# First layers and query/key projections in two halves of 256 columns in place of one matmul of 512

## Chip, cores and metric

One core of a Trainium2 chip runs the whole kernel. The metric is the device time of one execution in microseconds (us), lower is better; the number for the kernel before is the median of three runs. The profile is one further execution of the same program.

## What is computed

The input has 16 rows of 512 tokens with 256 features, float32. For each row:

```python
x = x + attn_block(layernorm(x))      # pre-norm attention, 16 heads of 16, window of 15 tokens, then a 256-1024-256 GELU layer
x = x + ffn_block(layernorm(x))       # main 256-1024-256 GELU layer, plus 2 of 8 experts (256-1024-256), chosen per row
# attn_block: qkv = h @ qkv_w + qkv_b ; windowed softmax(q k / 4) v ; @ proj_w
# ffn_block : a * main + (1 - a) * sum_k gate_k * (gelu(x @ W1e[k] + b1e[k]) @ W2e[k] + b2e[k])
```

So each row passes four two-layer networks of hidden width 1024: one in the attention block (kind "m" below) and three in the second block (kind "f": main and the two chosen experts).

## The kernel before

The program is written by hand, engine by engine, with semaphores. TensorE (PE) multiplies, ScalarE (ACT) applies GELU and rounds, VectorE (DVE) makes the low parts and does softmax and norms, GpSimd (POOL) splits the expert weights, SyncE (SP) issues the DMAs.

Precision: every float32 operand of a large product is kept as a pair, a rounded part `hi` and a rest `lo`, and each product is the sum of three matmuls, hi·hi, hi·lo and lo·hi (function `three`, L258 to L262; all large matmuls carry the line L261). Each matmul loads its stationary operand of 128 columns (LDWEIGHTS, rows "PEld") and streams its moving operand past it. In the trace a name such as `psB<-z_hi,wx_hi` gives the result, the moving and the stationary operand; for the second layers (`psB<-wx_hi,hr_hi`) the weights move and the hidden values are stationary.

The hidden width is cut into 32 chunks of 128 a row: 24 of kind "f" and 8 of kind "m". A written-out order (`ORDER`) runs, for slot q of a row, `chunk_up` of chunk q (first layer: 2 parts of the contraction x 3 products = 6 matmuls of 512 token columns into one PSUM bank) and then `chunk_down` of chunk q-2 (second layer: 4 groups of 128 tokens x 3 products = 12 matmuls with 256 weight columns moving). Between the two lie GELU (L984), rounding (L988) and the low part `hr_lo` (L632). The operands of the first layers are `zT` (kind "m") and `z3` (kind "f"); their weights are `wf1`, `wm1` and, for experts, a ring `wx` of four that POOL fills (L522, L524) from `raw`.

Between the chunks the order puts the attention of the row: `project_qk` (queries and keys, 4 per row, each 6 matmuls of 512 columns), `values` (12 matmuls of 256 columns in a half, `wv` moving), `scores` (L1272), transposes (L1161, L1289), `attend` (L1311) and `project` (24 matmuls of 256 columns, `wproj` moving). Three unused tensors (`shift_values`, `shift_z`, `shift_hr`, of 128, 64 and 224 bytes) move the addresses of what is allocated after them.

The change's and the prediction's steps touch `three`, `chunk_up`, `project_qk`, and, as neighbours on PE, `chunk_down`, `values` and `project`.

Of the kernel before, what the change touches and what calls it, by code (L numbers as in the profile page):

```python
# [5 lines left out]
P = 128  # L6
# [16 lines left out]
def build(nc, x, qkv_w, qkv_b, proj_w, proj_b, g1, b1, g2, b2, fc1_w, fc1_b, fc2_w, fc2_b,  # L23
# [4 lines left out]
    ROWS, T, D = x.shape  # L28
    HID = fc1_w.shape[1]
    E = w_gate.shape[1]  # L30
    KD, KH, NT = D // P, HID // P, T // P
# [32 lines left out]
    with ExitStack() as ctx:  # L64
# [3 lines left out]
        def pair(name, shape):  # L68
            return [sb(f"{name}_hi", shape, f32r), sb(f"{name}_lo", shape, f32r)]

        def signal(name, per=1, unit=1):
            return Signal(ctx.enter_context(nc.semaphore(f"s_{name}")), per, unit)
# [4 lines left out]
        wqk = pair("wqk", [P, KD, 2 * D])  # L77
# [19 lines left out]
        zT = pair("zT", [P, KD, T])  # L97
        z3 = pair("z3", [P, KD, T])
# [53 lines left out]
        psB = ctx.enter_context(nc.psum_tensor("psB", [P, 4, 512], f32))  # L152
        psA = ctx.enter_context(nc.psum_tensor("psA", [P, 4, 512], f32))
# [98 lines left out]

        router, lg_s, m8_s, idx_s, tw_s, tanh_s = (signal(n) for n in ("router", "lg", "m8", "idx", "tw", "tanh"))
        gate_s, b1x_in, b2x_in, b2_s = signal("gate", 2), signal("b1x_in", 2, 16), signal("b2x_in", 2, 16), signal("b2", 2)

        def split_value(n):
            return n + 1

        def three(eng, dst, a, b, start, stop):
            for n, (u, v) in enumerate(((0, 0), (0, 1), (1, 0))):  # L260
                last = eng.matmul(dst, a[u], b[v], start=start and n == 0, stop=stop and n == 2)  # L261
            return last  # L262

        def chunk_weights(m):
            if m < KH:
                return ([[w[:, k, m * P:(m + 1) * P] for w in wm1] for k in range(KD)], [w[:, m, :] for w in wm2])
            s = (m - KH) % RING
            return ([[w[:, s, k * P:(k + 1) * P] for w in wx] for k in range(KD)], [w[:, s, KD * P:] for w in wx])
# [42 lines left out]
        def fc(t, m):  # L311
            return CHUNK["f", t - 1, m]

        def mc(t, m):
            return CHUNK["m", t, m]
# [842 lines left out]
        def _(pe):  # L1158
# [4 lines left out]

            def chunk_up(t, kind, m):
                if kind == "m":
                    ps, z, off = psA, zT, 0
                    w1 = [[w[:, k, m * P:(m + 1) * P] for w in wf1] for k in range(KD)]
                    if m >= 2:
                        pe.wait_ge(gelu.sem, mc(t, m - 2) + 1)
                else:  # L1170
                    ps, z, off = psB, z3, 0
                    w1, _ = chunk_weights(m)
                    if m == 0:
                        pe.wait_ge(z3_lo.sem, z3_lo.all(t - 1))
                    if m >= KH:
                        pe.wait_ge(w_lo.sem, w_lo.at(t - 1, m - KH))
                    if m >= 2:
                        pe.wait_ge(gelu.sem, fc(t, m - 2) + 1)
                    elif t > 1:
                        pe.wait_ge(gelu.sem, fc(t - 1, NCH - 2 + m) + 1)  # L1180
                    elif m == 1:
                        pe.wait_ge(vs_s.sem, vs_s.all(1))
                for k in range(KD):
                    if kind == "m" and m == 0:
                        pe.wait_ge(t2_lo.sem, t2_lo.at(t, k))
                    last = three(pe, ps[:, m % 2, :], w1[k], [a[:, k, off:off + T] for a in z], k == 0, k == KD - 1)
                last.then_inc(up.sem, 1)

            def chunk_down(t, kind, m):
# [32 lines left out]
            def project_qk(t, c, which, bank):  # L1222
                col = which * D + c * P
                for k in range(KD):
                    if c == 0:
                        pe.wait_ge(t1_lo.sem, t1_lo.at(t, k))
                    last = three(pe, psA[:, bank, :], [w[:, k, col:col + P] for w in wqk], [z[:, k, :] for z in zT], k == 0, k == KD - 1)
                last.then_inc(qk.sem, 1)

            def values(t, n, parts=range(2)):  # L1230
# [123 lines left out]
            for h in range(2):  # L1354
                pe.wait_ge(z1_s.sem, z1_s.at(0, 2 * h + 1))
                for c in range(KD):
                    for i in HALVES[h]:
                        last = pe.transpose(psA[:, c, i * P:(i + 1) * P], tn[:, i, c * P:(c + 1) * P], ident[:, :])
# [10 lines left out]
            pe.wait_ge(p_lo.sem, split_value(2))  # L1369
            pe.wait_ge(small_t.sem, 1)  # L1370
            project_qk(0, 0, 0, 3)
            pe.wait_ge(p_lo.sem, split_value(3))
            project_qk(0, 0, 1, 2)
            values(0, 0)

            for t in range(ROWS + 1):
                f = t - 1
                for q in range(NQ + 2):
                    if q < NQ and there(ORDER[q][0], t):
                        chunk_up(t, *ORDER[q])  # L1380
# [14 lines left out]
                    elif q == 2:  # L1395
                        if t:
                            pe.wait_ge(vs_s.sem, vs_s.all(t))
                        else:
                            pe.wait_ge(kT_s.sem, kT_s.at(0, 0))
                        project_qk(t, 1, 1, 2)  # L1400
                    elif q == 3:
                        if t:
# [104 lines left out]
```

## Time and profile before

| | |
|---|---|
| median of 3 runs | 1864.18 us (1863.76 to 1865.44) |
| the profiled execution's own time | 1867.85 us |
| its span, first to last instruction | 1865.8 us |
| PE busy | 1851.9 us, 99% of the span |
| DVE, ACT, POOL busy | 1366.5, 1169.1, 870.2 us (73, 63, 47%) |
| PE matmuls, weight loads | 19591, 19591 |
| granted TensorE clock, mean | 0.998 of full speed |

Matmuls are pipelined: the duration of one in the profile (0.39 us for 512 columns, 0.28 us for 256) overlaps the next. What a matmul costs in a stream is the distance from its start to the next start, and that is read from the timeline.

### The profile page before, as it was taken

The page shows a single profiled execution, that of the slowest core. Times are in us where ns is not written, and L with a number is a line of the kernel's source. Part 1 is how long each engine was busy: PE and PEld are TensorE (multiplying, and loading weights), DVE is VectorE, ACT ScalarE, POOL GpSimd, SP SyncE. Part 2 cuts the span into 40 slices and gives each one's busy share as a digit, 9 for nine tenths or more (in the row PEclk, how much of TensorE's full clock was granted, in tenths as well). Part 3 has the DMA queues.
Part 4 walks back from the last instruction along what each step waited for, and adds up shares of the span by engine and source line. Part 5 has one row for each costly group of instructions (what it writes and reads, how often), then busy time and mean ns, then how long its engine had stood idle before and what let it go on. Part 6 is the DMA issues. An engine that isn't in the chain of part 4 may idle for free.

```text
span 1865.8 us, 49302 instructions
## 1 busy us (share of the span) xinstructions
PE 1851.9 (99%) x19591; PEld 1672.5 (90%) x19591; DVE 1366.5 (73%) x2226; ACT 1169.1 (63%) x1832; POOL 870.2 (47%) x788
## 2 busy tenths in 40 slices
PE   8999999999999999999999999999999999999999
PEld 7899898998989989899898998989999898999998
DVE  7677877778777686776867767687777877778644
ACT  6675665757557575665756657566575655657554
POOL 6545362552715437164362634636255371552725
PEclk9999999999999999999999999999999999999999
DMA  4231311303122032220313103131131311203121
GB/s 135 60 91 40 97 58 38 88 29 97 58 57 75 24 97 58 74 64 27 96 49 87 57 28 99 41 97 47 38 95 35 97 58 47 80 29 97 46 63 57
DMA packets 147437, 121.88 MB, mean 65 GB/s; under 512 B 17964, under 2 KB 139784, under 8 KB 147208
## 3 DMA queue, kind: packets, MB, share of 16 engines
q1 hardware_dynamic: 146512, 117.90, 22.1%
q8 instruction: 155, 2.54, 0.6%
q10 hardware_dynamic: 696, 0.83, 0.1%
q14 instruction: 74, 0.61, 0.1%
HBM read 85.52 MB, written 8.39 MB: 50 GB/s over the span
## 4 chain that ended last, share of the span: by engine, by line
PE 98%; DVE 1%; issue 0%; POOL 0%; DMA 0%; ACT 0%; SPq 0%; DVEq 0%; POOLq 0%; ACTq 0%
PE psB L261 58%; PE psA L261 28%; PE psA L1272 4%; PE psA L1289 3%; PE psA L1161 2%; PE psA L1311 2%; PE psB L1346 0%; PE psA L1327 0%; DMA xin<-in_L_attn_x 0%; POOL wf_lo L513 0%; DVE smax L745 0%; PE psB L1272 0%; PE psB L1289 0%; DVE smax L732 0%; DVE pr L749 0%
## 5 line engine op out<-in xcount | busy, mean ns | idle before, releaser
L632 DVE TENSOR_TENSOR hr_lo<-hf,hr_hi 128x512 fp32r<-128x512 f32 x512 | 504.6, 986 | 413.4 <-ACT hr_hi L988 413.1
L522 POOL TENSOR_SCALAR wx_hi<-raw 128x512 fp32r<-128x512 f32 x256 | 200.2, 782 | 650.8 <-DMA raw<-in_L_ffn_W2e 389.0
L988 ACT ACTIVATE hr_hi<-hf 128x512 fp32r<-128x512 f32 x512 | 323.4, 632 | 263.1 <-PE psB L261 179.9
L524 POOL TENSOR_TENSOR wx_lo<-raw,wx_hi 128x512 fp32r<-128x512 f32 x256 | 406.5, 1588 | 21.4
L984 ACT ACTIVATE hf<-psB,b1x 128x512 f32<-128x512 f32 x256 | 175.5, 686 | 178.1 <-PE psB L261 176.2
L261 PE MATMUL psB<-wx_hi,hr_hi 128*128 128x256 f32 x1016 | 283.8, 279 | 0.3
L261 PE MATMUL psB<-wx_hi,hr_lo 128*128 128x256 f32 x1016 | 281.5, 277 | 0.0
L261 PE MATMUL psB<-wx_lo,hr_hi 128*128 128x256 f32 x1016 | 281.5, 277 | 0.0
L261 PE MATMUL psB<-z_hi,wx_hi 128*128 128x512 f32 x512 | 212.1, 414 | 0.0
L261 PE MATMUL psB<-z_lo,wx_hi 128*128 128x512 f32 x512 | 201.7, 394 | 0.0
L261 PE MATMUL psB<-z_hi,wx_lo 128*128 128x512 f32 x512 | 201.5, 394 | 0.0
L261 PEld LDWEIGHTS psB<-wx_hi,hr_hi 128*128 128x128 f32 x1016 | 190.8, 188 | 11.6 <-DVE hr_lo L632 0.9
L261 PEld LDWEIGHTS psB<-wx_lo,hr_hi 128*128 128x128 f32 x1016 | 191.0, 188 | 8.8
L261 PEld LDWEIGHTS psB<-wx_hi,hr_lo 128*128 128x128 f32 x1016 | 190.7, 188 | 0.0
L984 ACT ACTIVATE hf<-psB,smallT 128x512 f32<-128x512 f32 x128 | 88.4, 690 | 120.3 <-PE psB L261 118.3
L461 POOL TENSOR_SCALAR ve<-mv 128x2 f32<-128x2 f32 (+1 forms) x94 | 25.2, 268 | 279.7 <-DVE mv L627 278.2
L261 PE MATMUL psA<-wf_hi,hr_hi 128*128 128x256 f32 x512 | 142.3, 278 | 0.0
L261 PE MATMUL psB<-wm_hi,hr_hi 128*128 128x256 f32 x512 | 142.2, 278 | 0.0
L261 PE MATMUL psA<-wf_lo,hr_hi 128*128 128x256 f32 x512 | 141.7, 277 | 0.0
L261 PE MATMUL psB<-wm_hi,hr_lo 128*128 128x256 f32 x512 | 141.7, 277 | 0.0
L261 PE MATMUL psA<-wf_hi,hr_lo 128*128 128x256 f32 x512 | 141.7, 277 | 0.0
L261 PE MATMUL psB<-wm_lo,hr_hi 128*128 128x256 f32 x512 | 141.7, 277 | 0.0
(213 smaller groups left out, 4646.2 us busy)
## 6 DMA issues: line engine op xcount, KB each, us to landing
raw<-in_L_ffn_W1e SPq DMA_DIRECT2D x256, 128.0 KB, 2.2
raw<-in_L_ffn_W2e SPq DMA_DIRECT2D x256, 128.0 KB, 2.2
vb<-vs SPq DMA_DIRECT2D x64, 192.0 KB
vb<-vs SPq DMA_DIRECT2D x64, 160.0 KB
out_x<-acc SPq DMA_DIRECT2D x31, 256.0 KB, 2.1
xin<-in_L_attn_x SPq DMA_DIRECT2D x15, 512.0 KB, 3.7
tm<-in_L_ffn_b2e SPq DMA_DIRECT2D x32, 128.0 KB, 3.0
raw<-in_L_attn_fc_w SPq DMA_DIRECT2D x8, 256.0 KB, 3.9
```

The costliest lines, as they stand in the source:

```text
L261: last = eng.matmul(dst, a[u], b[v], start=start and n == 0, stop=stop and n == 2)
L461: g.tensor_scalar(ve[:, j * NT + lo:j * NT + lo + w], mv[:, n, lo:lo + w, 1], a_, b_, ALU.mult, ALU.add).then_inc(vare[n].sem, 1)
L522: g.tensor_scalar(wx[0][:, s, :], raw[:, s, :], 1.0, 0.0, ALU.mult, ALU.add).then_inc(w_hi.sem, 1)
L524: g.tensor_tensor(wx[1][:, s, :], raw[:, s, :], wx[0][:, s, :].bitcast(f32), ALU.subtract).then_inc(w_lo.sem, 1)
L632: v.tensor_tensor(hr[1][:, c % 2, :], hf[:, c % 3, :], hr[0][:, c % 2, :].bitcast(f32), ALU.subtract).then_inc(h_lo.sem, 1)
L984: a.activation(hf[:, c % 3, :], src, func, bias=bias).then_inc(gelu.sem, 1)
L988: a.activation(hr[0][:, c % 2, :], hf[:, c % 3, :], ACT.Copy).then_inc(h_hi.sem, 1)
L1161: last = pe.transpose(psA[:, bank, i * P:(i + 1) * P], src[:, i, c * P:(c + 1) * P], ident[:, :])
L1272: last = pe.matmul(score_bank(t, u, gr)[cols, b * KW:(b + 1) * KW], qm[rows, th, b, cols], kT[rows, at:at + KW], start=t > 0, stop=t > 0 o ...
L1289: last = pe.transpose(turned_bank(t, h)[:, j * P:(j + 1) * P], unit(t, u)[:, 4 * h + j, :, :].rearrange("p g k -> p (g k)")[:, 0:PK], iden ...
L1311: last = pe.matmul(psA[cols, 2 + c, at:at + QB], vb[0:PK, j, 2 * th + h, w:w + G * HD], turned_unit(t, u)[0:PK, b, cols], start=True, stop ...
```

## The change

The first layers and the query/key projections stream their 512 token columns as two matmuls of 256, each with its own load of the stationary operand. For each part `k` of the contraction the three products are made for tokens 0 to 255 and then for tokens 256 to 511. Start and stop flags stand on the first and the last matmul of the bank; the semaphores, their places and every tensor's place stay. `values`, `project` and `chunk_down` are as they were.

```diff
+        def both_halves(eng, dst, a, z, k):
+
+            for h in range(2):
+                cols = slice(h * T // 2, (h + 1) * T // 2)
+                last = three(eng, dst[:, cols], a, [v[:, k, cols] for v in z], k == 0 and h == 0, k == KD - 1 and h == 1)
+            return last
...
             def chunk_up(t, kind, m):
                 if kind == "m":
-                    ps, z, off = psA, zT, 0
+                    ps, z = psA, zT
...
                 else:
-                    ps, z, off = psB, z3, 0
+                    ps, z = psB, z3
...
-                    last = three(pe, ps[:, m % 2, :], w1[k], [a[:, k, off:off + T] for a in z], k == 0, k == KD - 1)
+                    last = both_halves(pe, ps[:, m % 2, :], w1[k], z, k)
                 last.then_inc(up.sem, 1)
...
             def project_qk(t, c, which, bank):
...
-                    last = three(pe, psA[:, bank, :], [w[:, k, col:col + P] for w in wqk], [z[:, k, :] for z in zT], k == 0, k == KD - 1)
+                    last = both_halves(pe, psA[:, bank, :], [w[:, k, col:col + P] for w in wqk], zT, k)
                 last.then_inc(qk.sem, 1)
```

## Rows read from the trace of the kernel before

**Rows 1.** The page: busy us of each engine, share, instructions.
```profile
PE 1851.9 (99%) x19591; PEld 1672.5 (90%) x19591; DVE 1366.5 (73%) x2226; ACT 1169.1 (63%) x1832; POOL 870.2 (47%) x788
```

**Rows 2.** The page: the chain that ended last, by engine.
```profile
PE 98%; DVE 1%; issue 0%; POOL 0%; DMA 0%; ACT 0%; SPq 0%; DVEq 0%; POOLq 0%; ACTq 0%
```

**Rows 3.** Waits of PE: total us, times, longest; the two largest of nine.
```profile
PE psA L1358 <- DVE pr L602: 2.0, 2, 1.4
PE psB L1353 <- POOL ident L444: 1.9, 1, 1.9
```

**Rows 4.** Groups by line and shape, PE: one of three products of each.
```profile
L261 PE MATMUL psB<-z_hi,wx_hi 128*128 128x512 f32 x512 | 212.1, 414 | 0.0
...
L261 PE MATMUL psB<-z_hi,wm_hi 128*128 128x512 f32 x256 | 108.3, 423 | 0.2
...
L261 PE MATMUL psA<-zT_hi,wf_hi 128*128 128x512 f32 x256 | 100.8, 394 | 0.0
...
L261 PE MATMUL psA<-zT_hi,wqk_hi 128*128 128x512 f32 x128 | 50.6, 395 | 0.0
```

**Rows 5.** The chain in order of time: start, us, what.
```profile
273.26 1.39 PE psA L261 x6
274.64 1.37 PE psB L261 x12
276.02 16.56 PE psA L261 x108
```

**Rows 6.** Timeline, PE, a first layer, the second layer behind it, the next second layer.
```profile
1190.59 0.39 PE L261 MATMUL psA<-zT_hi,wf_hi 128*128 128x512 f32 x1
...
1191.97 0.28 PE L261 MATMUL psA<-wf_hi,hr_hi 128*128 128x256 f32 x1
1192.10 0.28 PE L261 MATMUL psA<-wf_lo,hr_hi 128*128 128x256 f32 x1
1192.21 0.28 PE L261 MATMUL psA<-wf_hi,hr_lo 128*128 128x256 f32 x1
1192.33 0.28 PE L261 MATMUL psA<-wf_hi,hr_hi 128*128 128x256 f32 x1
...
1193.35 0.39 PE L261 MATMUL psA<-zT_hi,wf_hi 128*128 128x512 f32 x1
...
1194.73 0.28 PE L261 MATMUL psA<-wf_hi,hr_hi 128*128 128x256 f32 x1
```

**Rows 7.** Timeline, PE, a whole projection (24) behind a second layer.
```profile
1167.09 0.28 PE L261 MATMUL psB<-wx_hi,hr_lo 128*128 128x256 f32 x1
...
1167.43 0.28 PE L261 MATMUL psB<-wx_hi,hr_lo 128*128 128x256 f32 x1
1167.55 0.28 PE L261 MATMUL psA<-wproj_hi,zT_hi 128*128 128x256 f32 x1
...
1170.37 0.40 PE L261 MATMUL psB<-z_hi,wx_hi 128*128 128x512 f32 x1
```

**Rows 8.** Timeline, PE, values (12) behind the scores.
```profile
200.88 0.38 PE L261 MATMUL psA<-wv_hi,zT_hi 128*128 128x256 f32 x1
201.10 0.28 PE L261 MATMUL psA<-wv_lo,zT_hi 128*128 128x256 f32 x1
201.22 0.28 PE L261 MATMUL psA<-wv_hi,zT_lo 128*128 128x256 f32 x1
201.33 0.28 PE L261 MATMUL psA<-wv_hi,zT_hi 128*128 128x256 f32 x1
...
202.35 0.39 PE L261 MATMUL psB<-z_hi,wm_hi 128*128 128x512 f32 x1
```

**Rows 9.** Timeline, DVE, around the same place as rows 6.
```profile
1191.51 2.54 DVE L632 TENSOR_TENSOR hr_lo<-hf,hr_hi 128x512 fp32r<-128x512 f32 x1 [0.28 <-ACT hr_hi L988]
1194.27 0.80 DVE L632 TENSOR_TENSOR hr_lo<-hf,hr_hi 128x512 fp32r<-128x512 f32 x1 [0.22 <-ACT hr_hi L988]
```

**Rows 10.** Groups, POOL: the split of the expert weights.
```profile
L524 POOL TENSOR_TENSOR wx_lo<-raw,wx_hi 128x512 fp32r<-128x512 f32 x256 | 406.5, 1588 | 21.4
L522 POOL TENSOR_SCALAR wx_hi<-raw 128x512 fp32r<-128x512 f32 x256 | 200.2, 782 | 650.8 <-DMA raw<-in_L_ffn_W2e 389.0 <-PE psB L261 260.9 <-PE psA L261 0.8
```

**Rows 11.** Timeline, PE, an attention product of many small matmuls.
```profile
905.88 1.15 PE L1272 MATMUL psA<-kT,qm 64*64 64x48 f32 x64
```

## The prediction

> **What bounds the kernel now.** I read the page first. PE is busy for 99% of the span [rows 1], and the chain that ended last is PE for 98% [rows 2]. So no transfer and no other engine sets the end; what one matmul costs in an unbroken stream does. The waits of PE say the same: the largest groups of them total 2.0 and 1.9 us, met twice and once [rows 3]. The profiled execution has a span of 1865.8 us and took 1867.85 us, 3.7 us over the median of 1864.18. I make the sum as a difference and set it against the median; 0.2% of that is 3.7 us, about what three runs can tell from no change.
>
> Busy times don't give the price of a matmul, since each overlaps the next (0.39 us for 512 columns). The price is the distance of starts. In the long stretch of chunks with nothing between them, 108 matmuls take 16.56 us [rows 5]. That is six pairs of a first layer (6 matmuls of 512 columns) and a second layer (12 of 256), so 16.56 / 6 = 2.76 us a pair, of which the chain gives 1.39 us to a first layer and 1.37 to a second [rows 5]. Thus 1.39 / 6 = 0.2315 us for 512 columns in a first layer. The second layer, from its fourth matmul on, goes at (1193.35 - 1192.33) / 9 = 0.1133 us for 256 columns [rows 6]. Two of these are 0.2267, which is 0.005 less than one of 512. This difference is the whole of the change, for better or worse.
>
> **What is removed and added.** Matmuls of 512 columns: each of the three products has 512 + 256 + 256 + 128 [rows 4], so 3456. They go, and 6912 of 256 columns come, each with its own load of 128 columns; weight loads rise from 19591 to 23047. No semaphore, tensor or DMA moves, and the number of columns streamed stays. These 3456 are 576 blocks of six: 512 first layers and 64 query/key projections.
>
> Issue and instruction supply: scores run 64 matmuls with 64 loads in 1.15 us [rows 11], 0.018 us for each, so the sequencer can feed one each 0.113 us; cost nothing. The extra loads lie under the streaming of the matmul before, as they do in the second layers, where a load belongs to each 256 columns. If that cover were gone, each would show as the first of the values behind the scores does: 0.22 us instead of 0.1133 [rows 8], 0.107 us each, or 3456 x 0.107 = 370 us. Nothing speaks for it: 0.1133 is reached wherever 256 columns move, for weights in the second layers and for `wv` in the values, (202.35 - 201.33) / 9 = 0.1133 [rows 6, 8].
>
> What no row shows is 256 columns of `z` moving past a first-layer weight. The nearest rows bound it.
> - From below: 0.1133 us, the settled second layer and the settled values. A block of 12 is then 1.36 us.
> - A second layer behind a first one doesn't start settled: its first three take 0.13, 0.11 and 0.12 [rows 6], and the 12 take about 1.375 us (1.37 in rows 5, 1.38 between the starts in rows 6). This entry cost of some 0.015 us may be one of leaving 512-column matmuls, and then goes away with them, or one of changing operands, and then comes at the first layers too.
> - From above: the projection. It too is 12 + 12 matmuls of 256 columns with the same kind of load, but its 24 take 1170.37 - 1167.55 = 2.82 us, 0.1175 each, and they never settle; the four second-layer matmuls in front of it go at (1167.55 - 1167.09) / 4 = 0.115 [rows 7]. A block of 12 is then 1.41 us.
>
> The break-even is 0.2315 / 2 = 0.1158 us, in the middle between the two. The row that it is nearest to is, I judge, the second layer. The kernel has pads of 128, 64 and 224 bytes that do nothing but shift tensors, so I compared places modulo 512 bytes, from the order and sizes of the allocations: a stationary operand lies 320 bytes (modulo 512) above the moving one in the second layers (`hr` against `w2`) and in the first layers (`w1` against `z`) alike, but 64 above in `values` and `project`. That first and second layers agree in this is a reason, not a proof: the settled values have the 64 as well and yet go at 0.1133.
>
> **The sum.** If the first layers take the second layers' whole-block time, 1.375 for 1.39, 576 x 0.015 = 9 us are saved. If everything settles at 0.1133, a pair is 24 x 0.1133 = 2.72 instead of 2.76, 512 x 0.04 = 20.5, and the 64 projections give 64 x 0.03 = 2, together 22 us. Nothing shows both entry costs gone, so I take a little less than the middle, 14 us: 1864 - 14 = 1850. The case's own range is 1842 to 1856.
>
> **Who else could take it back.** A pair shorter by 0.04 us must not run into its helpers. `hr_lo` is at times slow, 2.54 us from 1191.51 to 1194.05 [rows 9], and the second layer that needs it starts at 1194.73 [rows 6]: 0.68 us to spare. In the expert chunks POOL splits one weight piece per pair, 1.588 + 0.782 = 2.37 us [rows 10] of 2.72. Both stay hidden. What is late next would be `hr_lo`, once a pair were some 0.5 us shorter. The first layers' GELU waits for their last matmul as before.
>
> **The rivals.**
> - *The halves go at the projection's pace* (ends slower). Place: every first layer and query/key projection. Price: 12 x 0.1175 = 1.41 against 1.39, 0.02 us, up to 0.118 x 12 = 1.416 and 0.026, times 576 = 12 to 15 us, so 1876 to 1879. It decides from 0.1158 us a half on. For it: the projection is the only 256-column block that PE enters straight from a settled stream of 256 with the operands changing their parts, and so will every first layer be; the values that do settle come behind small matmuls and a load in the open. Against: the operands' distance above.
> - *The fixed price of a matmul.* The Trainium skill ("TensorE: Matmul & The Clock Gate", section "Wait — 56ns, not 53.3ns?") says that a warm matmul costs its columns at 2.4 GHz and about 2.5 ns fixed. By it the change would cost 3456 x 2.5 ns = 8.6 us and end at 1873, an estimate from the page. In rows: a fixed price f would make two halves 0.2315 + f. The settled ones give -0.005 and so deny it; the projection's, 2 x 0.1175 = 0.235, give +0.0035, 3456 x 0.0035 = 12 us. So as a mechanism of this kernel it joins the first rival, with 1872 to 1879 for both.
> - *Second layers lose too.* They are entered from 512-column matmuls now and settle from the slow side within three. Entered from 256-column ones they could stay at the projection's pace: 24 x 0.118 = 2.83 against 2.76, 0.07 x 512 = 37, so 1901.
> - *A wash.* Half of the blocks settle, or the entry cost comes twice: a pair of 2.755 to 2.765, within 4 us of 1864.
>
> **How the numbers follow.** Forecast (faster): 0.50. Wash: 0.12. The first two rivals together: 0.25. Second layers too: 0.13. The likeliest gives 1850. The range goes up to the first rival's end with a little for its size, 1882, and leaves the fourth case out (0.13); down to 1842, the bound with every half settled. Faster by over 0.2% 0.50, within 0.2% 0.12, slower 0.38.
>
> **What the profile after should show.** Matmuls 23047. Groups of z against weights at 128x256 with 1024 where 512 stood. In the stretch of six bare pairs, now 144 matmuls: 16.3 to 16.45 us if I am right; 16.7 with the first rival; 17.0 with the third. The distance of starts within a first layer should fall to 0.113 after at most three matmuls; 0.118 throughout would prove me wrong. No new wait of PE. The prediction goes wrong if the pace of 256 columns hangs on how a block is entered rather than on its operands.

## The result and the profile after

The changed kernel takes 1877.72 us (1877.62 to 1878.14, 3 runs) against 1864.18 us: ratio 1.0071, 95% interval 1.0054 to 1.0088. It is 13.5 us slower, where 14 us faster was forecast. The profiled execution took 1877.72 us, with a span of 1875.9 us. The spans differ by 10.1 us only, because the profiled execution of before was 3.7 us over its own median. Its granted clock over the first 70 us was 0.95, after the change 1.00, and I put the 3.7 us down to that.

The page of the changed kernel, against [rows 1]: PE is still the bound, and the matmuls and loads are 23047, as counted.

```profile
PE 1864.4 (99%) x23047; PEld 1840.1 (98%) x23047; DVE 1363.7 (73%) x2226; ACT 1168.3 (62%) x1832; POOL 866.4 (46%) x788
```

Its waits of PE (total us, times, longest), against [rows 3]; none lies in the steady part:

```profile
PE psA L1168 <- DVE tm L773: 2.1, 1, 2.1
PE psB L1360 <- POOL ident L451: 1.9, 1, 1.9
```

Its groups by line and shape, against [rows 4]; all first-layer matmuls have 256 columns (line 268 is line 261 of before):

```profile
L268 PE MATMUL psB<-z_hi,wx_hi 128*128 128x256 f32 x1024 | 295.5, 289 | 0.5 <-issue 0.5
```

Its chain in order of time, against [rows 5]. The stretch of six bare pairs, now 144 matmuls, is the same in every row of the input:

```profile
272.80 16.76 PE psA L268 x144
289.56 1.38 PE psB L268 x12
290.94 1.41 PE psA L268 x12
...
388.05 16.76 PE psA L268 x144
```

16.76 / 6 = 2.793 us a pair against 2.760. From one row of the input to the next it is 388.05 - 272.80 = 115.25 us; in the chain of before the stretch after the one at 276.02 [rows 5] is this:

```profile
390.35 16.56 PE psA L261 x108
```

390.35 - 276.02 = 114.33 us. The loss is 0.92 us a row of the input, 15 us for 16.

Where in the pair? The chain calls 12 matmuls 1.38 and 12 matmuls 1.41. The timeline tells which, against [rows 6]:

```profile
1200.71 0.28 PE L268 MATMUL psA<-wf_hi,hr_lo 128*128 128x256 f32 x1
1200.83 0.29 PE L268 MATMUL psA<-zT_hi,wf_hi 128*128 128x256 f32 x1
1200.95 0.28 PE L268 MATMUL psA<-zT_lo,wf_hi 128*128 128x256 f32 x1
1201.08 0.28 PE L268 MATMUL psA<-zT_hi,wf_lo 128*128 128x256 f32 x1
1201.19 0.28 PE L268 MATMUL psA<-zT_hi,wf_hi 128*128 128x256 f32 x1
...
1202.22 0.28 PE L268 MATMUL psA<-wf_hi,hr_hi 128*128 128x256 f32 x1
1202.33 0.28 PE L268 MATMUL psA<-wf_lo,hr_hi 128*128 128x256 f32 x1
...
1203.63 0.29 PE L268 MATMUL psA<-zT_hi,wf_hi 128*128 128x256 f32 x1
```

The first layer, which was changed, takes 1202.22 - 1200.83 = 1.39 us and no more than before. It starts with distances of 0.12, 0.13 and 0.11 and then goes at 0.113: (1202.22 - 1201.19) / 9 = 0.114. The second layer, in which no instruction was changed, takes 1203.63 - 1202.22 = 1.41 us instead of 1.375; after its first distance of 0.11 it goes at (1203.63 - 1202.33) / 11 = 0.118 to the end. In the whole trace, with the distances from each start to the next added up by kind of block, the 512 first layers went from 732.8 to 730.3 us, the 64 query/key projections from 89.3 to 88.1, and the 512 second layers from 711.9 to 729.7. That is -2.5, -1.2 and +17.8: together +14.1 us. What lies between the large products on PE (small matmuls and waits) went from 234.0 to 229.9 us, which fits the lower clock at the start of the one profiled execution of before; run 1 below, where it is unchanged too, has 229.5. So +14.1 in the blocks and 10.1 between the spans agree.

So a block of 256-column matmuls has two paces, 0.113 us ("settled") and 0.118 ("slow"), and the change put the second layers into the other. To count them I took the mean distance near the end of each block, below 0.115 settled, above 0.1165 slow. Before, 473 of 476 second layers behind a first layer of 512 columns were settled. After, of 408 second layers behind a settled first layer 407 were slow; of the 68 behind a slow first layer 51 were slow and 17 settled. In such counts below, of one block and the next, most cases with an idle gap between the two are left out, so the totals differ by a few.

### The profile page after: what moved, and what is told of

Its sections match the earlier page's. It is cut to its first block, busy times and chain, and to the rows that moved or that the text cites. A ratio compares the mean times of both kernels' runs of the same rounds, so it can differ in the third digit from the quotient of the medians.

```text
span 1875.9 us, 56214 instructions
## 1 busy us (share of the span) xinstructions
PE 1864.4 (99%) x23047; PEld 1840.1 (98%) x23047; DVE 1363.7 (73%) x2226; ACT 1168.3 (62%) x1832; POOL 866.4 (46%) x788
## 4 chain that ended last, share of the span: by engine, by line
PE 98%; DVE 1%; POOL 0%; issue 0%; DMA 0%; ACT 0%; SPq 0%; DVEq 0%; POOLq 0%; ACTq 0%
PE psB L268 58%; PE psA L268 28%; PE psA L1279 4%; PE psA L1296 3%; PE psA L1168 2%; PE psA L1318 2%; PE psA L1334 0%; DVE smax L752 0%; PE psB L1353 0%; DVE smax L739 0%; DMA xin<-in_L_attn_x 0%; DVE pr L756 0%; POOL band L495 0%; DVE st L629 0%; POOL rs L480 0%
## 5 line engine op out<-in xcount | busy, mean ns | idle before, releaser
L639 DVE TENSOR_TENSOR hr_lo<-hf,hr_hi 128x512 fp32r<-128x512 f32 x512 | 497.9, 973 | 432.8 <-ACT hr_hi L995 432.7
L529 POOL TENSOR_SCALAR wx_hi<-raw 128x512 fp32r<-128x512 f32 x256 | 192.8, 753 | 664.9 <-DMA raw<-in_L_ffn_W2e 393.4
L268 PE MATMUL psB<-z_hi,wx_hi 128*128 128x256 f32 x1024 | 295.5, 289 | 0.5 <-issue 0.5
L268 PE MATMUL psB<-wx_hi,hr_lo 128*128 128x256 f32 x1016 | 285.4, 281 | 0.0
L268 PE MATMUL psB<-z_lo,wx_hi 128*128 128x256 f32 x1024 | 285.2, 279 | 0.0
L268 PE MATMUL psB<-z_hi,wx_lo 128*128 128x256 f32 x1024 | 284.9, 278 | 0.0
L268 PEld LDWEIGHTS psB<-z_hi,wx_hi 128*128 128x128 f32 x1024 | 192.6, 188 | 3.1 <-issue 0.7
L268 PEld LDWEIGHTS psB<-z_lo,wx_hi 128*128 128x128 f32 x1024 | 193.1, 189 | 0.0
L268 PEld LDWEIGHTS psB<-z_hi,wx_lo 128*128 128x128 f32 x1024 | 192.7, 188 | 0.0
L268 PE MATMUL psB<-z_hi,wm_hi 128*128 128x256 f32 x512 | 149.8, 293 | 0.2
```

What stands on the lines that cost most here:

```text
L529: g.tensor_scalar(wx[0][:, s, :], raw[:, s, :], 1.0, 0.0, ALU.mult, ALU.add).then_inc(w_hi.sem, 1)
L639: v.tensor_tensor(hr[1][:, c % 2, :], hf[:, c % 3, :], hr[0][:, c % 2, :].bitcast(f32), ALU.subtract).then_inc(h_lo.sem, 1)
```

## The experiments

Each was timed in the same job as the kernel before, and each verdict is read against the kernel before in that job. For the pace within the pair I show, for most runs, the stretch of six bare pairs from the chain of the trace: before and in run 1 16.56, changed 16.76 us. The theories are named by letters in the expectations, each where it first comes up.

**1. Only the projections halved.** `chunk_up` as before, `project_qk` as changed.

```diff
-                    last = both_halves(pe, ps[:, m % 2, :], w1[k], z, k)
+                    last = three(pe, ps[:, m % 2, :], w1[k], [a[:, k, :] for a in z], k == 0, k == KD - 1)
```

> Only the 64 query/key projections are halved (384 more matmuls), the first layers stay at 512 columns. Theory A (what a block of 256-column matmuls costs is decided by what it is entered from; a second layer entered from a settled 256-column stream stays at 0.118 us): no second layer is entered from a halved block here, the halved projections take 1.36 to 1.38 us instead of 1.39 to 1.40, so about 1862.5. Theory B (each added matmul and load costs the same, 13.5 us / 3456 = 3.9 ns): 384 x 3.9 ns = 1.5 us more, 1865.7.

1865.52 us, ratio 1.0005 (0.9995 to 1.0014). The time can't tell the theories apart, the trace can. The timeline of one projection behind a second layer:

```profile
889.95 0.28 PE L268 MATMUL psB<-wm_hi,hr_lo 128*128 128x256 f32 x1
890.06 0.28 PE L268 MATMUL psA<-zT_hi,wqk_hi 128*128 128x256 f32 x1
...
891.47 0.40 PE L268 MATMUL psB<-z_hi,wm_hi 128*128 128x512 f32 x1
```

12 matmuls take 891.47 - 890.06 = 1.41 us; the same 12 take this long in the changed kernel:

```profile
896.20 0.28 PE L268 MATMUL psA<-zT_hi,wqk_hi 128*128 128x256 f32 x1
...
897.57 0.28 PE L268 MATMUL psB<-z_hi,wm_hi 128*128 128x256 f32 x1
```

1.37 us. The instructions, operands and places are the same. What differs is the second layer in front: settled in the first, slow in the second. My expectation of 1.36 to 1.38 us was wrong, and the way in which it was wrong points to the cause: a halved projection too is slow when it is entered from a settled second layer (45 of 45 here), and it settles when it is entered from a slow one (45 of 45 in the changed kernel). The 64 projections went from 89.3 to 90.5 us, the second layers stayed at 712.1.

**2 and 3. Half of the halving, at the front or at the end of the block.** Both have 5184 first-layer-like matmuls (9 a block), and differ only in which part of the contraction is whole.

```diff
         def both_halves(eng, dst, a, z, k):
+            if k == KD - 1:
+                return three(eng, dst, a, [v[:, k, :] for v in z], False, True)
```

is run 2; run 3 has instead

```diff
+            if k == 0:
+                return three(eng, dst, a, [v[:, k, :] for v in z], True, False)
```

> In every first layer and projection the first part of the contraction is halved, the last part is whole again: 3 of 6 matmuls halved, the block ends in 512 columns. Theory A: the second layers behind settle again, 1.37 us instead of 1.41, and the total is 1864 within 4 us. Theory B: half of the added matmuls, half of the loss, 1871.

> The mirror of the run before: the first part of the contraction is whole, the last part halved, so the block ends in six matmuls of 256 columns; as many matmuls in all. Theory A: the second layers stay at 0.118 us as in the changed kernel, 512 x 0.038 = 19 us lost there, first layers about as before: 1878 to 1884. Theory B: 1871, the same as its mirror.

Run 2 (ends in 512 columns): 1868.68 us, ratio 1.0019 (1.0010 to 1.0029). Run 3 (ends in 256): 1882.85, ratio 1.0100 (1.0083 to 1.0117). The chains:

```profile
272.94 16.68 PE psA L270 x126
```

```profile
273.44 16.88 PE psA L270 x126
```

The same number of matmuls, loads and columns, and 14 us between them. A fixed price for each added matmul can't do that. Run 2 lies 3.7 us over the kernel before; run 3 is inside the 1878 to 1884 of theory A, though not quite as it had it: the second layers lost 14.8 us, not 19, and the first layers 3.4 (736.2), not nothing. The trace of run 2 has its second layers back at 711.8 us in all, that of run 3 at 726.7. In run 2 I had the second layers right (1.372 us each) and the first layers wrong: entered from a settled block, their halves are slow (0.118, the projections' lesson again), and they add up to 736.2 us, 3.4 more than before.

**4. The place of `hr`.** The changed kernel, with another pad ahead of `hr`.

```diff
-        shift("hr", 224)
+        shift("hr", 96)
```

> The changed kernel with the pad ahead of hr at 96 bytes instead of 224: hr (stationary in the second layers) then lies 192 instead of 320 bytes (modulo 512) above the weights that move, and at the same place modulo 512 as z. Theory A in its bare form (only the entry counts, not the places of the operands): 1877.7, second layers at 0.118 us. Rival C (the places decide whether a stream settles): another pace of the second layers, from 0.1133 us, 1858, to 0.122, 1900.

The pad moves `hr` and with it all that is allocated after it (identity, masks, biases, statistics). Of these a second layer reads only `hr`; its weights lie ahead of the pad and stay.

1869.98 us, ratio 1.0025 (1.0015 to 1.0035): 128 bytes give back 8 of the 13 us. The bare form of theory A falls. Its stretch of bare pairs:

```profile
273.19 16.70 PE psA L268 x144
```

The timeline of two pairs:

```profile
1190.57 0.28 PE L268 MATMUL psA<-zT_hi,wf_hi 128*128 128x256 f32 x1
...
1191.99 0.28 PE L268 MATMUL psA<-wf_hi,hr_hi 128*128 128x256 f32 x1
...
1193.40 0.28 PE L268 MATMUL psA<-zT_hi,wf_hi 128*128 128x256 f32 x1
...
1194.78 0.28 PE L268 MATMUL psA<-wf_hi,hr_hi 128*128 128x256 f32 x1
...
1196.14 0.28 PE L268 MATMUL psA<-zT_hi,wf_hi 128*128 128x256 f32 x1
```

One pair is slow in both blocks, 1.42 + 1.41 us, the next is settled in both, 1.38 + 1.36. Every second pair is so. Here a second layer takes the pace of the first layer in front of it (settled after settled 269 times, slow after slow 205 times, against it 2 times), and a first layer behind a second takes the other pace (142 settled to slow, 87 slow to settled; 20 against). With the old pad a first layer took the other pace than the second in front (settled behind slow 231 of 232, slow behind settled 19 of 19), and a settled first layer was followed by a slow second; only slow first layers left their second layers slow more often than not (51 of 68). So the entry decides and the places decide what the entry does: theory A and rival C were each half right.

**5. Whole at both ends.** First and last of six products 512 columns, the four between halved.

```diff
+            if k == 0 or k == KD - 1:
+                out = []
+                for n, (u, j) in enumerate(((0, 0), (0, 1), (1, 0))):
+                    if n == (0 if k == 0 else 2):
+                        out.append(eng.matmul(dst, a[u], z[j][:, k, :], start=k == 0, stop=k == KD - 1))
+                        continue
...
```

> Of the six products of a first layer or projection the first and the last are whole (512 columns), the four between are halved: 8 matmuls of 256. Theory D (each block of 256-column matmuls is either at 0.113 or at 0.118 us; a whole matmul ahead of it lets it settle at 0.113, a change of operands without one passes the pace on or turns it over): both second layers and the halves inside the first layers settle, 0.23 + 8 halves with an entry of 0.012 + 0.23 = 1.38 us for a first layer, 1.372 for a second, so 1864 - 512 x 0.01 = 1859. Theory B (each added matmul costs 3.9 ns): 2304 x 3.9 ns = 9 us, 1873.

1879.16 us, ratio 1.0076 (1.0060 to 1.0093). Theory D's claim that one whole matmul lets the next block settle is wrong. 255 of 476 second layers behind a whole last matmul were slow. The state went through the one whole matmul in both directions: the halves of a first layer took the pace of the second layer in front (slow behind slow 164 times, settled behind settled 85 times, never otherwise), and a second layer took mostly the other pace than the halves in front (slow behind settled 207 of 209, settled behind slow 221 of 269). In the timeline, the starts of five blocks:

```profile
1198.15 0.28 PE L278 MATMUL psA<-wf_hi,hr_hi 128*128 128x256 f32 x1
...
1199.53 0.39 PE L262 MATMUL psA<-zT_hi,wf_hi 128*128 128x512 f32 x1
...
1200.90 0.28 PE L278 MATMUL psA<-wf_hi,hr_hi 128*128 128x256 f32 x1
...
1202.32 0.40 PE L262 MATMUL psA<-zT_hi,wf_hi 128*128 128x512 f32 x1
...
1203.73 0.28 PE L278 MATMUL psA<-wf_hi,hr_hi 128*128 128x256 f32 x1
```

A settled second layer (1.38 us, its entry included) is followed by a settled first layer (1.37), that by a slow second layer (1.42), and that by a slow first layer (1.41). With three whole matmuls (run 2) or six (before) at this place of `hr` the second layers settled; two were not tried. The time is 6 us over theory B's 1873, and runs 2 and 3 have already ruled B out.

**6 to 8. The place of `z`.** The changed kernel with the pads ahead of `z` and `hr` at 192 and 96, 192 and 224, 128 and 160 bytes.

```diff
-        shift("z", 64)
+        shift("z", 192)
...
-        shift("hr", 224)
+        shift("hr", 96)
```

The diff is that of run 6; run 7 keeps 224 for `hr`, run 8 has 128 and 160. What lies between the two pads (the operands of the attention and `hf`) moves with `z`.

> The changed kernel with the pad ahead of z at 192 bytes (64 before) and the pad ahead of hr at 96 (224 before): z moves by 128 bytes, hr stays where it was. Theory D: hr against z now stands as in the run with the shifted hr (the same modulo 128 and 256), so first layers at 0.113 are followed by second layers at 0.113; whether the other change of operands, second to first layer, stops turning the pace over is what this run asks. If it does, both settle and the time is 1842 to 1850; if not, half of the blocks are slow, 1868 to 1872. If only the place of hr against its weights counted, which is the changed kernel's own here, 1877.

> The same move of z by 128 bytes, and hr moves with it (pad 224), so the distance from z to hr is the changed kernel's. Theory D with the distance from z to hr as what turns the pace at a second layer: second layers behind settled first layers go at 0.118 again, 1877 if the other change of operands still turns the pace, about 1870 to 1900 if it doesn't and one slow state lasts. If the distance of hr to its weights decides instead (here that of the run with shifted hr, modulo 256 by 128 from the changed kernel's), 1870 or less.

> z moved by 64 bytes only, hr where it was. Theory D has no row for a step of 64. If places count in steps of 128 bytes and a half step matters not, the first layers and second layers behave as in the changed kernel or as in the run before, 1842 to 1878; if 64 bytes bring the two streams into each other's way, the settled pace itself goes up, above 0.115 us everywhere, 1880 to 1900.

1876.13 us, ratio 1.0065 (1.0048 to 1.0082); 1893.14, 1.0151 (1.0134 to 1.0168); 1909.17, 1.0239 (1.0222 to 1.0256). Their chains, one each:

```profile
273.06 16.70 PE psA L268 x144
```

```profile
276.54 16.96 PE psA L268 x144
```

```profile
277.35 17.12 PE psA L268 x144
```

Run 6 is run 4 mirrored: a first layer keeps the pace of the second in front (247 of 249), a second layer turns it over (settled to slow 167 of 167; slow to settled 223, slow to slow 85). Its bare pairs cost the same 16.70; behind small matmuls it does worse, with 166 of 182 first layers slow where the changed kernel has 47. In run 7 no second layer settled at all, 16.96 / 24 / 6 = 0.1178 us throughout the stretch. Run 8 shows that 64 bytes do more than turn a pace: first layers go at 0.120 us, and all 476 second layers behind them are slow. At 1909.17 it is 9 us above the highest outcome that I gave as possible, 1900.

**9. Runs 3 and 4 together.** First part whole, last halved, `hr` at a pad of 96.

> Two runs put together: the first part of the contraction whole, the last halved (there the first layers settled at 0.113 us whether the block before was settled or not, and the second layers then went at 0.118), and hr at a pad of 96 bytes (there a settled first layer was followed by a settled second layer). Theory E (each block is settled or slow; what makes it one or the other is the block before it together with the places of the operands, and both effects add up as measured): first layers 0.694 + 0.691 = 1.385 us, second layers 1.362, a pair 2.747 against 2.760, so 1864.5 - 512 x 0.013 = 1858. Theory B (a fixed price of 3.9 ns for each added matmul): 1871. If the two don't add up: 1870 to 1883.

1864.20 us, ratio 0.9997 (0.9988 to 1.0007). No difference, where 1858 was expected. The bare pairs did what was expected:

```profile
272.04 16.44 PE psA L270 x126
```

16.44 / 6 = 2.740 us (2.747 expected). But the first layers right behind a settled query/key projection went slow (30 of 30), those behind scores did in 30 of 46 cases, and with this pad a second layer keeps what it finds: 133 of them were slow behind slow first layers. The gain of 512 columns turned into 256 is real where it isn't lost at a neighbour.

**10. The kernel before with the pad at 96.** Nothing halved.

> The kernel before with nothing changed but the pad ahead of hr, 96 bytes for 224. Theory E: second layers entered from 512-column blocks settle at either place; their entry of 0.122, 0.116, 0.114 is what may change, by up to 0.012 us each, so 1858 to 1866. If the place of hr itself costs or saves by the block, whatever it is entered from: outside of that.

1888.56 us, ratio 1.0134 (1.0117 to 1.0151). Outside of what theory E expected:

```profile
275.00 16.88 PE psA L261 x108
```

The timeline, a second layer between two first layers:

```profile
1191.37 0.28 PE L261 MATMUL psB<-wx_hi,hr_hi 128*128 128x256 f32 x1
...
1192.79 0.39 PE L261 MATMUL psB<-z_hi,wx_hi 128*128 128x512 f32 x1
...
1194.18 0.28 PE L261 MATMUL psB<-wx_hi,hr_hi 128*128 128x256 f32 x1
```

1.42 us for the second layer, 1.39 for the first. 475 of 476 second layers are slow now, from the same blocks of 512 columns behind which 473 of 476 settled with the pad at 224. The pad of before fits blocks of 512 columns ahead of the second layers; with the halved blocks the other is better by 8 us (run 4). So 8 of the 13 us lost go with a layout that fits the other shape.

**11. Whole at both ends, pad at 96.**

> The run with whole matmuls at both ends of a first layer, with hr at a pad of 96 bytes. There a block passed its state on to the next one (a settled second layer to a settled first layer 85 of 85 times, a slow one to a slow one 164 of 164). Theory E: the place of hr acts at the first matmul of a second layer alone, which is entered from a whole one here; if it leaves the passing-on as it is, 1875 to 1881; if it lets the second layers settle always, 1858.

1877.37 us, ratio 1.0072 (1.0055 to 1.0088), inside the first band, but not by passing on: 474 of 476 second layers were slow (as in run 10: they come behind a whole matmul) and 309 of 310 first layers and query/key projections that follow a second layer or the output projection were settled.

**12. Each slot as it measured best.** Pad 96. 13 of the 32 slots are all halved: ten behind small matmuls and three right behind a query/key projection. The other 19 have their first part whole: 15 right behind a second layer, the rest behind scores, values, transposes or the output projection.

```diff
+        OPEN = [("f", m) for m in (3, 4, 5, 6, 7, 8, 9, 11, 12, 13, 17, 21, 23)]
+
+        def both_halves(eng, dst, a, z, k, first_whole):
+            if first_whole and k == 0:
+                return three(eng, dst, a, [v[:, k, :] for v in z], True, False)
...
-                    last = both_halves(pe, ps[:, m % 2, :], w1[k], z, k)
+                    last = both_halves(pe, ps[:, m % 2, :], w1[k], z, k, t == ROWS or (kind, m) not in OPEN)
```

> The pad ahead of hr at 96 bytes; a first layer or projection that comes right behind a second layer has its first part of the contraction whole and the last halved, one that comes behind small matmuls or another first-layer-like block (13 of the 32 slots, and the second of two projections in a row) is all halved. From the slots of the two runs that did each thing everywhere, theory E (the state of a block is made by the block before it and by the places, nothing else) sums, against the kernel before, to 0.67 us a row in these slots and 0.06 us in the projections: 16 x 0.7 = 11 to 12 us, 1853. Theory B (3.9 ns for each added matmul): 1873. If the blocks behind a different neighbour than in those two runs fall back to 0.118 us, 1860 to 1870.

1855.93 us, ratio 0.9947 (0.9934 to 0.9961): 9.1 us faster than the kernel before in that job (1864.99), some 22 us below the changed one, with 2361 matmuls more than before. The page, and the stretch of bare pairs:

```profile
PE 1841.4 (99%) x21952; PEld 1770.8 (96%) x21952; DVE 1374.1 (74%) x2226; ACT 1168.1 (63%) x1832; POOL 868.5 (47%) x788
```

```profile
271.46 16.44 PE psA L271 x126
```

Its first layers add up to 726.4 us, its second layers to 710.0, the projections to 88.1; 422 of 436 second layers behind settled first layers settled. Two slots fell back against what they had in the runs that they were taken from, the 12th (its second layer 1.43 us instead of 1.37) and the 18th (1.50 + 1.42 instead of 1.46 + 1.36), which is most of the 2 to 3 us that are missing. I took each slot's choice from two runs, so the parts of its gain are fitted, but the total was expected ahead of the run (1853) and measured (1855.93).

## Why the prediction was wrong

- *PE bounds, nothing else takes it back*: right. PE 99% busy, no new wait, `hr_lo` and the weight splits stayed hidden.
- *Counts, issue and hidden loads*: right. 23047 matmuls, no load in the open in the steady part.
- *The nearest row for a halved first layer is the second layer*: right in the pace, wrong in the sum. First layers behind a second layer settle at 0.113 from the fourth or fifth matmul on, as the second layers did. But the entry cost came along: 1.383 us a block (median, behind a second layer) against 1.388, so 2.5 us were saved in all 512, where the lower term of the sum had 9 and the forecast 14. Only behind a settled query/key projection is the entry cost gone, 1.364 against 1.397.
- *A second layer stays as it is or loses its entry cost*: this is the step that failed. In the forecast it stood as "This entry cost ... may be one of leaving 512-column matmuls, and then goes away with them, or one of changing operands, and then comes at the first layers too". The sum took at most 1.375 us for a second layer. There was a third outcome: behind 512-column matmuls, at this place of `hr`, the second layer settles after a short slow entry; entered from settled 256-column matmuls it starts quicker (0.114) and then stays at 0.118: 1.410 instead of 1.372, 0.038 x 512 = 19 us by medians, 17.8 in the whole trace. The last sentence of the prediction named this as the way to go wrong, and it is what happened.
- *The rivals*. The first named 1876 to 1879, and 1877.72 was measured, but in the wrong place: it let the first layers go at the projection's pace, and most don't (98 of 512 are slow). That its number was met is luck, and so is that the bare stretch, 16.76 us, lies at the 16.7 named as its sign. (The 1872 to 1879 given for the first two rivals together has no row of this case for its low end; the rows give 1876.) Its reason was the right one ("the only 256-column block that PE enters straight from a settled stream of 256 with the operands changing their parts"); I applied it to the blocks that were changed and not to those behind them. The fourth case had the second layers slow, but only together with the first layers, and so priced it at 1901. The rows held it: the projection comes right behind a settled block and is slow [rows 7], the values come behind small matmuls and settle [rows 8]. I named this as the rival's reason and gave the difference of places more weight. The hint was weaker than it looks now: in the changed kernel the projection is slow behind slow second layers as well (15 of 15), so its own pace does not turn with the block in front.
- *The addresses*. The argument from distances modulo 512 was a weak reason for the forecast. Places do matter: with only pads changed the changed kernel runs from 1870 to 1909 us (runs 4, 6, 7, 8) and the kernel before at 1889 instead of 1864 (run 10). But equal distance from stationary to moving operand didn't make the blocks equal.
- *The fixed price of a matmul*: runs 2 and 3 have equally many matmuls and took 1868.68 and 1882.85 us, and run 12 has 2361 more than before and is faster. A fixed price alone explains none of these. The 2.5 ns that the Trainium skill ("TensorE: Matmul & The Clock Gate", section "Wait — 56ns, not 53.3ns?") gives as the fixed part would have made it 1873, an estimate from the page, which these runs don't bear out.

**What is shown and what stays open.** Shown: the loss sits in the unchanged second layers; the pace of a block depends on the block before it, with the same instructions and places (runs 1 and 2 against 3); pads of 128 bytes change what is passed on (runs 4, 6, 7, 10), and one of 64 changes the pace itself (run 8). Each place was tried once, and a pad moves all that lies behind it, so which distance counts isn't separated. Not shown: what the state is in the hardware. The records of the weight loads don't tell: in both paces nearly every load is recorded 2 to 4 ns after the start of a matmul. In settled first and second layers no load lasts 192 ns (nearly all 187 or 188); in slow ones of the changed kernel about three in ten do, and in run 8 nearly all of the first layers', but in the slow blocks of run 7 none. I can't predict from the pads which way a change of operands turns: runs 1, 5, 6, 9 and 10 came out otherwise than expected, run 8 lay outside its bands, and run 11 fell into its band for another reason.

## What to carry to other kernels

In a stream in which PE is never idle, a few ns on each matmul are the whole budget, and the price of a block may sit in the block behind it: before halving or reordering anything, read start distances of the unchanged neighbours in each way in which they are entered today. A layout tuned by pads is tuned for the shapes around it; change the shape and the pads must be measured again, both together. And where two forms of a block each win behind different neighbours, choose per slot from two traces instead of one form for all (run 12).

## What the runs showed of the hardware

- Matmuls of 256 columns with a load each run back to back at 0.113 or at 0.118 us for a whole block of 12, with the same instructions and places (run 1 against the changed kernel), and keep the pace where the next block has the same kind of operands (settled query/key projection to settled first layer, 44 of 44 in the changed kernel). Two of them at 0.113 are cheaper than one of 512 at 0.2315.
- A pad of 128 bytes less ahead of the stationary operand of the second layers, with no instruction changed, costs 24 us, 1.3% (run 10). A shift by 64 bytes of `z`, moving in the first layers, gives a third pace, 0.120 us (run 8).
- Three or six whole matmuls of 512 columns ahead of a second layer let it settle at one place of `hr` (before, run 2); one doesn't reliably (run 5, 255 of 476 slow), and at the other place of `hr` six don't either (run 10).
